# A product moved from VectorE to GpSimd in a ternary feed-forward

## The reference

```
def bitlinear(x, w, g):                    # per token
    xn = x * rsqrt(mean(x*x) + 1e-6) * g
    scale = 127 / clip(max|xn|, 1e-5)
    xq = clip(round(xn * scale), -128, 127) / scale
    return xq @ ternary(w).T
h = gelu(bitlinear(x, w1, g1))             # 192 -> 768 features
out = bitlinear(h, w2, g2)                 # 768 -> 192 features
```

## Time and profile before

| | us |
|---|---|
| median of 3 runs | 1861.83 (1856.94 to 1866.59) |
| the profiled execution | 1866.93 |
| its span, first to last instruction | 1865.1 |
| TensorE busy | 1593.4 (85%) |
| VectorE busy | 1286.3 (69%) |
| ScalarE busy | 997.8 (54%) |
| GpSimd busy | 123.4 (7%) |

### The profile page before, as it was taken

One profiled execution on the slowest core, in us unless ns is written; L12 is line 12 of the kernel. 1 busy time (PEld: TensorE's weight loads), 2 busy tenths in 40 slices (PEclk: granted clock), 3 DMA queues, 4 the chain that ended last, 5 costly groups with the idle time before them and its releaser, 6 DMA issues. The chain is left out here.

```text
span 1865.1 us, 26108 instructions
## 1 busy us (share of the span) xinstructions
PE 1593.4 (85%) x9615; PEld 875.6 (47%) x9615; DVE 1286.3 (69%) x3014; ACT 997.8 (54%) x1429; POOL 123.4 (7%) x159
## 2 busy tenths in 40 slices
PE   3778788989999999984477887898999999999836
PEld 2457465652343333372234664756433334333814
DVE  7767742148998899736966777402589999895477
ACT  1533533145777777843552345221467777777355
POOL 6010000000000000005201000000000000000010
PEclk9888899998999999996687889699989999999957
DMA  7005200043000100001000241000620000000001
GB/s 159 0 10 155 65 9 1 1 135 110 27 26 26 33 28 27 1 1 32 20 17 1 69 117 52 1 0 0 186 68 27 26 27 26 26 27 1 1 1 34
DMA packets 53859, 73.35 MB, mean 39 GB/s; under 512 B 18647, under 2 KB 27172, under 8 KB 53734
## 3 DMA queue, kind: packets, MB, share of 16 engines
q1 hardware_dynamic: 52198, 68.55, 12.9%
q0 software_dynamic: 1536, 3.15, 0.7%
HBM read 38.51 MB, written 33.17 MB: 38 GB/s over the span
## 5 line engine op out<-in xcount | busy, mean ns | idle before, releaser
L1267 ACT ACTIVATE Er<-ST 128x1024 f32<-128x1024 f32 x384 | 377.0, 1021 | 107.8 <-PE ST L892 107.5
L1670 DVE TENSOR_REDUCE nmp<-S 128x1 f32<-128x512 f32 x514 | 337.7, 683 | 31.5 <-PE S L858 31.4
L892 PE MATMUL ST<-QS,KS 100*128 100x512 bf16 x768 | 218.8, 387 | 0.3
L908 PE MATMUL PV<-Er,V 128*17 128x512 f32 x1536 | 212.4, 602 | 0.0
L858 PE MATMUL S<-KS,QS 96*128 96x512 bf16 x514 | 183.4, 392 | 2.3 <-DMA QS<-scr_q 1.5
L1670 DVE TENSOR_REDUCE nmp<-MT 128x1 f32<-128x512 f32 x254 | 173.6, 683 | 13.5 <-PE MT L858 13.5
L858 PEld LDWEIGHTS S<-KS,QS 96*128 96x128 bf16 x514 | 48.2, 98 | 156.4 <-DVE nmp L1670 104.1
L449 POOL TENSOR_SCALAR tp<-mv 128x8 f32<-128x8 f32 x20 | 5.5, 275 | 1621.3 <-DVE mv L1470 1620.0
L892 PEld LDWEIGHTS ST<-QS,KS 100*128 100x128 bf16 x768 | 72.5, 99 | 64.7 <-issue 5.9
L1618 DVE TENSOR_REDUCE nmp<-S 128x1 f32<-128x512 f32 x120 | 77.5, 684 | 36.1 <-PE S L674 35.9
L858 PE MATMUL MT<-KS,QS 96*128 96x512 bf16 x254 | 99.4, 391 | 0.9 <-DVE nmp L1670 0.9
(11 more groups left out here) (396 smaller groups left out, 3014.1 us busy)
## 6 DMA issues: line engine op xcount, KB each, us to landing
KS<-scr_k SPq DMA_DIRECT2D x72, 192.0 KB, 2.6
scr_k<-R SPq DMA_DIRECT2D x16, 576.0 KB, 4.0
QS<-scr_q SPq DMA_DIRECT2D x48, 192.0 KB, 2.9
scr_k<-R SPq DMA_DIRECT2D x16, 384.0 KB, 4.6
QS<-scr_k SPq DMA_DIRECT2D x24, 192.0 KB, 2.5
scr_q<-R SPq DMA_DIRECT2D x8, 576.0 KB, 4.6
scr_k<-R SPq DMA_DIRECT2D x16, 192.0 KB, 5.2
scr_q<-R SPq DMA_DIRECT2D x8, 384.0 KB, 4.8
```

The costliest lines, as they stand in the source:

```text
L892: ins = nc.tensor.matmul(ST[i % 2][:, (kt % 2) * HALF:(kt % 2 + 1) * HALF], KS[0:KP + 4, k, kt * P:(kt + 1) * P], QS[0:KP + 4, k, half * H ...
L908: ins = nc.tensor.matmul(PV[row:row + VC, :], slots[h // H].V[:, kt, h % H, :], E[:, step % RING, (kt % 2) * HALF:(kt % 2 + 1) * HALF], st ...
L1267: A_(E[:, g, :], ST[i % 2][:, :], ACT.Exp).then_inc(s["exps"], 1)
L1670: v.tensor_reduce(nmp[:, u // 2, u % 2:u % 2 + 1], bank, AX.X, ALU.max).then_inc(s["reduced"], 1)
```

## The change

The in-place product by `g2bc` leaves VectorE's `spread` and is done by GpSimd, tile by tile, `a` and `z` in turn, four tiles of each slot before the rsqrt of that half. A new semaphore `weighed` of each slot counts its tiles, and VectorE's reduction waits for it. The rsqrt's own wait on `hss` goes, since the wait of the last product covers it. The product, its operands and its shape stay as they were.

```diff
 OWN = """... bhid bgelu hss weighed hrms ...""".split()

 # GpSimd
                 for half in range(2):
+                    for t in range(HT * half, HT * half + HT):
+                        for o in slots:
+                            g.wait_ge(o.s["hss"], p * 8 + t + 1)
+                            g.tensor_tensor(o.HG[:, t % HT, :], o.HG[:, t % HT, :], g2bc[:], ALU.mult).then_inc(o.s["weighed"], 1)
                     for o in slots:
                         h = slice(HT * half, HT * half + HT)
-                        g.wait_ge(o.s["hss"], p * 8 + HT * half + HT)
                         link(g.tensor_scalar(o.tp[:, h], o.ss[:, h], 1.0 / F, None, ALU.mult))
                         rsqrt(o, o.rn[:, h], o.tp[:, h], RMS_EPS, h).then_inc(o.s["hrms"], 1)

 # VectorE
             def spread(p, o, t):
-                ve.wait_ge(o.s["hss"], p * 8 + t + 1)
-                link(v.tensor_tensor(o.HG[:, t % HT, :], o.HG[:, t % HT, :], g2bc[:], ALU.mult))
+                ve.wait_ge(o.s["weighed"], p * 8 + t + 1)
                 link(v.tensor_reduce(o.amax[:, t:t + 1], o.HG[:, t % HT, :], AX.X, ALU.max, apply_absolute_value=True))
```

More of the change, by code:

```diff
@@ L166, in build @@
         OWN = """gathered stats rstd xnorm turned evac inproj inproj_out conv silu dterm gated proj hi resid mid lo vproj vcopied
-            hidden gelu ffn h2 bhid bgelu hss hrms hquant hturned hcopied bout outs stored kw0 kw1 qw0 qw1""".split()
+            hidden gelu ffn h2 bhid bgelu hss weighed hrms hquant hturned hcopied bout outs stored kw0 kw1 qw0 qw1""".split()
         slots = []
```

## The result

The changed kernel takes 1885.5 us (median, 1881.68 to 1888.03), the kernel before 1861.52 beside it; the ratio is 1.012, 95% interval 1.0084 to 1.0156. It is slower by about 1.2%, and 1884 was predicted. The profiled execution took 1888.03 us with a span of 1886.2, 21.1 over before's span.

The account below looks back on a forecast made before the run. VectorE was taken to bound the feed-forward stage. Pass 0's 15.7 us (9.3 + 4.8 + 0.5 + 1.1) and pass 1's 6.6 (1.3 + 4.8 + 0.5) gave +22.3, so 1884.1 us; range 1877 to 1891, 8 in 10 for 1868 to 1896.

Parts of the forecast that it names:

- a product, start to start: GpSimd's 768-column product: 1.75 us plus 0.08 between operations, one each 1.83 us, a little slower than ScalarE's 1.76.
- pass 0, first half: Eight products queue behind the last gather, two rsqrt behind them; scales of z end at 905.3 against 895.97: +9.3 us.
- pass 1, first half: No gathers; products trail ScalarE and the rsqrt stands behind them; scales end at 1816.4 against 1815.09: +1.3 us.
- middles: Second halves, tiles 2 and 3: quantises on VectorE wait for running GpSimd products; +4.8 us in each pass.
- ends: Second halves, last square to next quantise: product, two rsqrt, scales, +0.5 us each pass; pass 0's memset adds +1.1.
- sum: Whole kernel: pass 0's 15.7 us and pass 1's 6.6 us, together +22.3 us.
- the memset's row: Profile row: qinv, normally 0.17 us, stood until GpSimd's memset ended; taken as the case for every TENSOR_SCALAR meeting a product.
- without turns: Middle of second halves without the lock between VectorE's quantises and GpSimd's products: would end at 19.95 us, -0.3.
- No blocking: Rival, middle of second halves: quantises run beside GpSimd's products; sum 12.1 us, so 1874; chance 0.14.
- cheap product: Rival: a GpSimd product takes 0.9 us, so not slower; sum -0.2 us, 1862; chance 0.10.
- dear: Rival: a GpSimd product takes 2.2 us and bounds both first halves; sum 33.6 us, so 1895; chance 0.12.

Follow-up runs that it names:

- memset early: Kernel before, with GpSimd's memset of QS for pass 1 issued ahead of the last two inverse_deviation of pass 0; 1864.9 us, ratio 0.9995.
- before, plain quantise: Kernel before, both quantise operations in a form that also sums its output (accum_out), rounding left out; 1890.1 us, ratio 1.0119.
- idle, two inputs: Kernel before plus unused GpSimd products for every squared tile, reading two different tensors (g2bc and wf2); one execution, 1891.3 us.
- after, plain quantise: Changed kernel, both quantise operations in a form that also sums its output (accum_out), rounding left out; 1889.0 us, ratio 1.0124.
- second halves only: Changed kernel with products on GpSimd for tiles 4 to 7 only, tiles 0 to 3 on VectorE as before; 1876.6 us, ratio 1.0075.
- idle products: Kernel before plus an unused GpSimd product of g2bc with itself for every squared tile, ahead of each half's rsqrt; 1893.1 us, ratio 1.0135.

## Why the prediction was right

| step | predicted | measured |
|---|---|---|
| a product, start to start | 1.83 | 1.76 |
| pass 0, first half | +9.3 | +7.3 (but see below) |
| pass 1, first half | +1.3 | +0.9 |
| middles | +4.8 each | +5.0, +4.8 |
| ends | +1.6, +0.5 | +1.5, +0.5 (behind the last square +1.1, +0.5) |
| sum | +22.3 | +20.0 |

- **Pass 0's first half** has the mechanism that was named: gathers, then eight products, then two rsqrt, then the scales. It was over-sized by 2.0 us against the trace. The gathers took 19.9 us in place of 21.3: in the earlier trace rows they run beside VectorE's products, in the changed kernel beside nothing. I had taken the old end for the new one. The products' rate of 1.76 and the rsqrt's 1.69 give the rest. And the reference isn't clean: the trace of before holds a wait of ScalarE of 2.6 us there whose releaser the profile doesn't know:

```profile
883.80 0.90 ACT L1303 ACTIVATE R<-ST,gsc 128x768 f32<-128x768 f32 x1 [2.60 <-remote]
```

  The "memset early" run (30.19) and "before, plain quantise" (29.72) have one too, and "idle, two inputs" and "after, plain quantise" hide one behind GpSimd; "second halves only", the same code up to there, has none and needs 28.07. Against that, the change costs 9.5 us and the whole sum is 22.2. That these fall so near the predicted 9.3 and 22.3 is partly luck: the forecast set the new first quantise 2.0 us too late, and the old one that it was taken from was late by the wait, 2.2 us. What makes the wait is open. None of the three traces with early gathers has it, and five of the nine with late ones do.
- **Pass 1's first half** has the mechanism that was named: the rsqrt behind the products is what `scales` wait for, by 0.70 and 0.64 us in the trace. The last 0.4 us of the forecast was the products' rate.
- **The middles** went by the memset's row, taken as the case for every fast VectorE operation. The runs with idle products and with plain quantises show that it holds for the quantises, and that the dependency costs nothing: -1.2 us without turns, where I had -0.3 (with quantises that are themselves 0.4 us slower). The steps fell as named: counted from the first quantise, the product of `z` tile 4 ended at 10.1 us (10.0 named), tile 6 of `a` was squared at 20.6 (19.2 or 20.9), and the middle ended at 25.1 (25.0). Two sizes were off and cancelled: without turns it is 0.9 us shorter than named, and four waits of about 1.5 us make 6.1 where the forecast held 5.1. The operations lasted 2.04 to 2.18 us in place of about 0.6.
- **The ends:** from the last square to the next quantise pass 1 took 6.44 us, 6.4 named. `qinv` of `z` lasted 3.32 us (3.5 named), and no quantise of the last four tiles was stretched. In pass 0 this part grew by 1.1 us and not 1.6; the other 0.4 of the measured 1.5 lie ahead of the last square, where equal work varies by 0.9, and aren't the change's for sure.
- **Rivals.** "No blocking" and "cheap product" fell with the stretched rows and the 1.76; the "dear" one too. The timed medians differ by 24 us, 4 more than the stages hold; the interval of the ratio is 16 to 29 us, so those 4 aren't shown to be there.

## What to carry to other kernels

An idle engine in the busy table isn't free time. Before moving work onto it, look at what its queue holds when the work comes due, at what stands behind the work in that queue, and at whose operations can't run beside it. VectorE's share of busy time fell and the kernel got slower, partly because its fast single-input operations, the ones that look cheapest, are those that a GpSimd operation kept waiting here. That is half of the 20 us; the rest is the order of GpSimd's own queue.

## What the runs showed of the hardware that I had not expected

- A GpSimd product that reads the same tensor for both inputs took 1.47 us undisturbed and kept VectorE's two-input product off for 1.18 us; with two different tensors it kept it off for 1.52 us. Whether the same address or the same tensor counts wasn't tried.
- VectorE lost its fast form to `accum_out`: 768 columns took 953 to 1008 ns in place of 560 to 615, and such an operation ran beside a GpSimd product without a stretch.
- The turns go both ways: in the run with two different inputs both engines went on by one VectorE product (0.96 us) and one hold by GpSimd's (1.52) at a time, 2.48 us in all, and VectorE's reduction (0.95) ran inside that hold.
- Indirect gathers from GpSimd follow each other by 1.25 us. 16 of them took 19.9 us while VectorE stood idle, 21.3 beside its products in the kernel before, and 22.7 in "second halves only", where the last three each began just inside a two-input product of VectorE and lasted 1.68 us. GpSimd above, VectorE below:

```profile
878.97 1.68 POOL L471 DMA_INDIRECT U<-_L_tok_embed_matrix_dram,tok_i  x1 [0.30 <-issue]
```

```profile
878.87 0.96 DVE L1736 TENSOR_TENSOR R<-R,g2bc 128x768 f32<-128x768 f32 x1
```
